# Layer norm of the feed-forward samples by products with a constant tile in place of transposes and batch-norm statistics

## The chip, the cores and the metric

The kernel runs on one core of one Trainium2 chip. The metric is device time in microseconds for one execution. A profile of one execution shows how long each engine worked and what it waited for: TensorE (PE; PEld is its weight load), VectorE (DVE), ScalarE (ACT), GpSimd (POOL) and SyncE (SP), which issues the transfers.

## The reference

A stack of four layers works on x of shape (8, 512, 512): a rotation of columns, a conditioned two-matrix block, a low-rank addition, and a transformer layer. The change lies in the second layer norm of the transformer layer, ahead of its feed-forward part:

```python
def layernorm(x, gamma, beta):
    mu = jnp.mean(x, axis=-1, keepdims=True)
    var = jnp.var(x, axis=-1, keepdims=True)
    return (x - mu) * jax.lax.rsqrt(var + EPS) * gamma + beta
...
x1 = x + attn_out
h2 = layernorm(x1, gamma2, beta2)
ff = jax.nn.gelu(h2 @ W1 + b1, approximate=False) @ W2 + b2
x2 = x1 + ff
g = gate_score[:, None, None]
return x + g * (x2 - x)
```

For each sample there are 512 tokens of 512 features, and the feed-forward part has 2048 hidden features.

## The kernel before

A sample lies in SBUF by features: 128 partitions, J = 4 tiles of 512 tokens, so that feature sums run over the partitions and the tiles. The first third of the run is the conditioned block, the middle is attention of all eight samples, and from about 925 us on only the feed-forward part of the samples is left. The code numbers samples from 0. Sample 0 uses a plain first product, the others (1 to 7) seven block products in place of eight (`product`, `PRODUCTS`), each of two times three passes in 128x256 pieces. The norms that the change touches are those of samples b = 2 to 7, the third to the eighth.

The work of one sample is cut into eight **periods**, p = 0 to 7. In one period TensorE issues, in this order: products 1 and 6 of the next pair of hidden tiles, `second_product` of the first hidden tile on output tiles 0 and 1, product 7, the same `second_product` on tiles 2 and 3, products 4 and 5, `second_product` of the other hidden tile on 0 and 1, products 2 and 3, and `second_product` on 2 and 3. Each half of a `second_product` is six 128x512 matmuls (L83 to L85, the helper `three_pass`). Each engine has its queue in program order, and semaphores tie them. Up to sample 2's statistics and norm the order is written out by hand, one call per line, for each engine; from then on it is the functions `period` in a loop over b = 2 to 7, which prepare sample b + 1 inside sample b.

Between the products of a pair and its `second_product` lies a chain over two engines. DVE adds the products (`partial_of`, L2237). ScalarE applies Gelu (`pair_high`, L2398) and rounds a copy to the matmul's type (L2401). DVE subtracts to get the low part (`pair_low`, L2216). `second_product` waits for that subtraction. `pair_high(n + 1, True)` waits for the fourth partial, `partial_of(n + 1, 3)`; a `product(·, 7)` waits for all five partials of the pair before, and a `product(·, 4)` for the first of its own pair.

The norm of sample b + 1 goes like this. In p = 1 DVE starts the result (`start_result`, L2156) and GpSimd adds a bias to it (L2097). In p = 2 DVE adds the attention result to x (`add_attention`, L2144). At the end of p = 2 and in the middle of p = 3 TensorE transposes x in sixteen 128x128 pieces (`tokens`, L2451) into the two PSUM banks `turn(0)` and `turn(1)`, DVE takes `bn_stats` and `bn_aggr` of each of four token tiles (`statistics`, L2164 and L2166), and GpSimd makes the reciprocal root of four columns by a power of minus a half (L2100, L2102). In p = 4 TensorE spreads mean and reciprocal root over the partitions by eight transposes (`spread`, L2467 and L2471), and DVE subtracts the mean (`centre`, L2177). In p = 5 DVE multiplies by the reciprocal root (`normalise`, L2183), ScalarE scales (`scale`, L2354), and both split the blocks for the products.

For b = 2 the same steps stand in the hand-written queues. ScalarE's is, around the change:

```python
ff.factor_high(6, 0)
ff.pair_high(3, True)
ff.factor_high(6, 1)
...
ff.pair_high(4, False)
ff.factor_high(7, 0)
ff.factor_high(7, 1)
ff.scale(2, 0)
ff.pair_high(5, True)
ff.scale(2, 1)
ff.copy_first(6)
```

`factor_high(6, 0)` and `factor_high(7, 0)` wait for a transfer of weights.

Of the kernel before, what the change touches and what calls it, by code (L numbers as in the profile page):

```python
# [18 lines left out]
P = 128  # L19
# [1906 lines left out]
def feed_forward_engines(nc, ctx, io, keep, psum, attention):  # L1926
# [29 lines left out]
    whole_tile = keep["stack_f"][1][:, 7, :]  # L1956
    partial = rows_of(keep["raw"][:, 2:4, :, :])[:, 6:8, :].rearrange("p n (h s) -> p (n h) s", h=2)
# [16 lines left out]
    added, summed, biased, gated = sem("added"), sem("summed"), sem("biased"), sem("gated")  # L1974
    given_ld, factor_sum, factor_hi, factor_lo = sem("given_ld"), sem("factor_sum"), sem("factor_hi"), sem("factor_lo")
# [30 lines left out]
    made_of = lambda part: given[part[1]][:, :, part[2], :].rearrange("p k a c -> p a k c")  # L2006

# [85 lines left out]
    def gpsimd(pool):  # L2093
        for b in range(B):
# [3 lines left out]
            if b + 1 < B:  # L2098
                pool.wait_ge(mv_set, T * (b + 1))
                pool.tensor_scalar(var[:], mv[:, :, 1], LN_EPS, None, ALU.add).then_inc(var_set, 1)  # L2100
                pool.wait_ge(var_set, b + 1)
                pool.tensor_tensor(rstd[:], var[:], keep["minus_half"][:], ALU.pow).then_inc(rstd_set, 1)  # L2102

    def vector(dve):
# [54 lines left out]
        def statistics(b, t):  # L2159
            if b == 1:  # L2160
                dve.wait_ge(tok_set, t + 1)
            else:
                dve.wait_ge(tin_full, T * (b - 1) + t + 1)
            dve.bn_stats(st[:, t, :], tok[:, t, :] if b == 1 else turn(t)).then_inc(stat_set, 1)  # L2164
            dve.wait_ge(stat_set, T * (b - 1) + t + 1)
            dve.bn_aggr(mv[:, t, :], st[:, t, :]).then_inc(mv_set, 1)  # L2166

# [6 lines left out]
        def centre(b):  # L2174
            dve.wait_ge(tback_full, J + 2 * (b - 2) + 1)
# [71 lines left out]
        def period(b, p):  # L2247
# [7 lines left out]
            if more and p == 3:  # L2255
                statistics(b + 1, 0)
                statistics(b + 1, 1)
# [15 lines left out]
            if more and p == 2:  # L2273
                add_attention(b + 1)
            if more and p == 5:
# [8 lines left out]
            if more and p == 3:  # L2284
                statistics(b + 1, 2)
                statistics(b + 1, 3)
# [21 lines left out]
        return steps(w1_low, w2_low, factor_low, factor_sums, add_attention, start_result, statistics, normalise_first, block_low, block_sums,  # L2308
                     split, finish, pair_low, partial_of, centre, normalise, samples)

    def scalar(act):
# [29 lines left out]
        def tokens(t):  # L2341
# [3 lines left out]
            act.activation(tok[:, t, :], turn(t), ACT.Copy).then_inc(tok_set, 1)  # L2345

# [56 lines left out]
        def period(b, p):  # L2403
# [29 lines left out]
        return steps(w1_high, w2_high, factor_high, tokens, scale, block_high, gelu, copy_first, pair_high, samples)  # L2433

    def tensor(pe):
        def tokens(b, t):
            if t == 0:
                pe.wait_ge(mid_set, J * b)
                if b == 1:
                    attention["results_taken"](pe)  # L2440
                elif b == 2:
                    pe.wait_ge(h_set, J)
                else:
                    pe.wait_ge(normed, T + 2 * J * (b - 2))
# [2119 lines left out]
```

## Time and profile before

| | us |
|---|---|
| median of three runs | 1609.24 |
| the three runs | 1609.21, 1609.24, 1613.74 |
| span of the profiled execution | 1610.9 |
| TensorE busy in it | 1585.8 (98%) |
| VectorE, ScalarE, GpSimd busy in it | 1166.6, 982.8, 410.9 |
| one steady sample (1213.0 to 1299.6) | 86.6 |

The profile gives the span from the first to the last instruction, 1610.9 us, and no separate time for what lies around it. It is 1.7 us above the median and between the runs shown. In a row of the timeline the first number is the start in us, the second the duration; x4 is four instructions shown as one row. Matmuls overlap in the records, so their pace is read from start to start.

### The profile page before, as it was taken

Reading aid. Unit: us, or ns where it says so; the run is one execution under the profiler, and the core shown is the slowest. Engines: PE = TensorE matmul, PEld = TensorE weight load, DVE = VectorE, ACT = ScalarE, POOL = GpSimd, SP = SyncE. Lnnn points to the kernel's source line nnn. Section 1 sums busy time; section 2 is a strip of 40 time slices with the busy share of each in tenths; the row PEclk is TensorE's granted clock in tenths of the full one; section 3 lists DMA queues with packets and bytes.
Section 4 is the critical chain, followed back from the end, with each engine's and each line's share of the span. In section 5 each row is a group of like instructions: output and inputs, shape, how many; then the busy total and the mean of one; then the engine's idle time right before and its main releaser. Section 6 shows DMA issues by size and latency. Waiting matters only on the chain.

```text
span 1610.9 us, 27177 instructions
## 1 busy us (share of the span) xinstructions
PE 1585.8 (98%) x9296; PEld 1299.5 (81%) x9298; DVE 1166.6 (72%) x2767; ACT 982.8 (61%) x2331; POOL 410.9 (26%) x605
## 2 busy tenths in 40 slices
PE   7999999999999999999999999999999999999999
PEld 4688786777777777777777688898999999999998
DVE  7999888786969686868778576785655656565643
ACT  6888766887878787878778755352433324242422
POOL 8998810313222313131312110201010110202010
PEclk8999999999999999999999999999999999999999
DMA  7042135543545444444337435866464555556361
GB/s 308 0 183 97 66 126 126 149 130 92 138 95 139 100 115 122 111 116 115 88 90 214 167 152 207 303 262 232 178 234 170 213 225 188 212 178 265 142 211 68
DMA packets 62257, 254.79 MB, mean 158 GB/s; under 512 B 10628, under 2 KB 16004, under 8 KB 46760
## 3 DMA queue, kind: packets, MB, share of 16 engines
q1 hardware_dynamic: 62120, 253.06, 48.2%
q8 instruction: 74, 1.21, 0.3%
q14 instruction: 63, 0.52, 0.1%
HBM read 153.93 MB, written 48.23 MB: 125 GB/s over the span
## 4 chain that ended last, share of the span: by engine, by line
PE 90%; POOL 3%; DMA 2%; DVE 2%; ACT 1%; issue 1%; SPq 1%; POOLq 0%; DVEq 0%; ACTq 0%
PE psum L83 24%; PE psum L84 23%; PE psum L85 23%; PE psum L1529 5%; PE psum L1549 5%; PE psum L1579 4%; PE psum L1470 1%; DMA k_weights<-w_factors 1%; PE psum L1478 1%; PE psum L2451 1%; DMA k_raw<-in_t_w 1%; POOL k_gs_square L252 1%; POOL k_gs_root L247 1%; ACT psum L1229 1%; POOL k_gs_scaled L256 1%
## 5 line engine op out<-in xcount | busy, mean ns | idle before, releaser
L1229 ACT ACTIVATE psum<-psum,b_mx 128x512 f32<-128x512 f32 (+3 forms) x512 | 258.9, 509 | 63.2 <-DVE b_mx L990 62.0
L990 DVE CUSTOM_DVE_ANT_0 psum<-psum,b_mask 128x512 f32<-128x512 f32 (+3 forms) x512 | 244.7, 506 | 53.0 <-PE psum L1529 48.1
L2398 ACT ACTIVATE k_act<-k_stack_f,k_smalls 128x512 f32<-128x512 f32 x112 | 80.9, 722 | 303.6 <-DVE k_stack_f L2237 297.1
L1241 ACT ACTIVATE k_exps<-psum 128x512 f32<-128x512 f32 (+1 forms) x384 | 194.6, 532 | 59.4 <-PE psum L1549 58.1
L864 POOL TENSOR_SCALAR_AFFINE_SELECT k_exps<-k_exps 128x256 f32<-128x256 f32 x256 | 96.4, 413 | 381.0 <-ACT k_exps L1241 379.1
L2097 POOL TENSOR_SCALAR k_result<-k_result,k_pb 128x512 f32<-128x512 f32 x32 | 59.2, 1866 | 434.9 <-DVE k_result L2156 434.9
L2216 DVE TENSOR_TENSOR k_act_lo<-k_act,k_act_hi 128x512 fp32r<-128x512 f32 x112 | 77.2, 690 | 120.6 <-ACT k_act_hi L2401 120.6
L83 PE MATMUL psum<-k_act_hi,k_w_hi 128*128 128x512 f32 x384 | 150.8, 393 | 0.0
L84 PE MATMUL psum<-k_act_lo,k_w_hi 128*128 128x512 f32 x384 | 150.5, 392 | 0.0
L85 PE MATMUL psum<-k_act_hi,k_w_lo 128*128 128x512 f32 x384 | 150.2, 391 | 0.0
L2237 DVE TENSOR_TENSOR k_raw<-psum,k_raw 128x256 f32<-128x256 f32 x168 | 70.5, 421 | 106.0 <-PE psum L85 95.4
L1529 PE MATMUL psum<-k_stack 96*128 96x512 f32 (+3 forms) x512 | 142.6, 330 | 3.1 <-DMA k_stack<-k_samples 2.0
L85 PE MATMUL psum<-k_normed,k_weights 128*128 128x512 f32 (+1 forms) x384 | 144.3, 376 | 0.0
L1549 PE MATMUL psum<-k_stack 98*128 98x512 f32 (+3 forms) x512 | 134.8, 332 | 0.6 <-ACT k_exps L1241 0.3
L83 PE MATMUL psum<-k_normed,k_weights 128*128 128x512 f32 (+1 forms) x320 | 126.0, 394 | 0.0
L84 PE MATMUL psum<-k_normed,k_weights 128*128 128x512 f32 (+1 forms) x320 | 120.0, 375 | 0.0
L1529 PEld LDWEIGHTS psum<-k_stack 96*128 96x128 f32 x512 | 93.6, 190 | 29.9 <-issue 8.8
L1549 PEld LDWEIGHTS psum<-k_stack 98*128 98x128 f32 x512 | 91.0, 189 | 27.7 <-issue 9.6
L1229 ACT ACTIVATION_READ_ACCUMULATOR psum<-psum,b_mx 128x1 f32 x512 | 108.6, 212 | 0.0
L85 PEld LDWEIGHTS psum<-k_act_hi,k_w_lo 128*128 128x128 f32 x384 | 72.1, 188 | 16.2
L85 PEld LDWEIGHTS psum<-k_normed,k_weights 128*128 128x128 f32 x384 | 73.0, 190 | 14.1
L83 PE MATMUL psum<-k_h,k_stack 128*128 128x256 f32 x294 | 82.6, 281 | 0.0
(372 smaller groups left out, 4418.2 us busy)
## 6 DMA issues: line engine op xcount, KB each, us to landing
k_stack<-w_factors SPq DMA_DIRECT2D x35, 1792.0 KB, 7.7
k_stack<-k_samples SPq DMA_DIRECT2D x384, 128.0 KB, 2.4
k_weights<-w_factors SPq DMA_DIRECT2D x17, 1792.0 KB, 7.5
x<-k_tokens SPq DMA_DIRECT2D x10, 1024.0 KB, 4.3
k_tokens<-x SPq DMA_DIRECT2D x8, 1024.0 KB, 5.1
d<-k_result SPq DMA_DIRECT2D x32, 256.0 KB, 2.9
k_raw<-x SPq DMA_DIRECT2D x8, 1024.0 KB, 4.8
k_raw<-d SPq DMA_DIRECT2D x8, 1024.0 KB, 7.1
```

Source lines behind the costliest of these rows:

```text
L83: pe.matmul(out, w_hi, x_hi, start=start and k == 0, stop=False)
L84: pe.matmul(out, w_hi, x_lo, start=False, stop=False)
L85: last = pe.matmul(out, w_lo, x_hi, start=False, stop=stop and k == n - 1)
L864: pool.affine_select(out=own, in_=own, compare_op=ALU.is_ge, fill=0.0, base=0, pattern=[[0, 2], [1, P]], channel_multiplier=-1).then_inc(c ...
L990: last = dve.tensor_tensor_reduce(got, got, mask[:, S - width:S], -INV_SQRT_DH, -2.0 * MASKED, ALU.add, ALU.min, mx[n % 2][:, h, t:t + 1])
L1229: act.activation(sc(n, u)[:, at:at + width], sc(n, u)[:, at:at + width], ACT.Exp, bias=mx[n % 2][:, h, t:t + 1], scale=-1.0, accum_out=sum ...
L1241: act.activation(exps[n % 2][:, h, at:at + width], by_key(n, u)[:, 0:width], ACT.Exp, scale=INV_SQRT_DH).then_inc(k_act, 1)
L1529: last = pe.matmul(sc(n, u)[:, at:at + width], stack[n % 2][0:3 * DH, 2 * h, t * P:(t + 1) * P], stack[n % 2][0:3 * DH, 2 * h + 1, 0:width ...
L1549: last = pe.matmul(by_key(n, u)[:, at:at + width], stack[n % 2][0:3 * DH + 2, 2 * h + 1, j * P:(j + 1) * P], stack[n % 2][0:3 * DH + 2, 2 ...
L2216: dve.tensor_tensor(act_lo[n % 2], act_f[:], act_hi[n % 2].bitcast(F32), ALU.subtract).then_inc(act_lo_set, 1)
L2237: dve.tensor_tensor(out, got, other, ALU.add).then_inc(partial_set, 1)
L2398: act.activation(act_f[:], whole_tile, ACT.Gelu, bias=small(smalls, "b1", 2 * pair % M + second)).then_inc(pair_gelu, 1)
```

## The change

For samples b = 2 to 7 the transposes and the batch-norm statistics go. GpSimd adds the four tiles of x, splits the sum into a high and a low part (`token_sum`), and TensorE multiplies both with a constant tile of 1/512, which gives the mean, already on all partitions, in `turn(0)` (`mean_product`). ScalarE squares the four tiles of x (`squares`), GpSimd adds the squares and splits the sum (`square_sum`), TensorE multiplies again (`square_product`, `turn(1)`). ScalarE squares the mean, DVE makes the variance, ScalarE takes Ln and Exp of it for a rough reciprocal root, and DVE refines that in three instructions. All of this works on 128x512 elements where the statistics before had a column for each token tile.

```diff
 def gpsimd(pool):
+        def token_sum(b):
+            pool.wait_ge(mid_set, J * (b - 1) + 2)
+            pool.tensor_tensor(sum_f, x[:, 0, :], x[:, 1, :], ALU.add).then_inc(sums_set, 1)
+            for j in (2, 3):
+                pool.wait_ge(mid_set, J * (b - 1) + j + 1)
+                wait_sums(pool, b, j - 1)
+                pool.tensor_tensor(sum_f, sum_f, x[:, j, :], ALU.add).then_inc(sums_set, 1)
+            wait_sums(pool, b, 3)
+            pool.tensor_copy(sum_hi, sum_f).then_inc(sums_set, 1)
+            wait_sums(pool, b, 4)
+            pool.tensor_tensor(sum_lo, sum_f, sum_hi.bitcast(F32), ALU.subtract).then_inc(sums_set, 1)
+
+        def square_sum(b):
+            wait_squares(pool, b, 1)
+            pool.tensor_tensor(tok[:, 0, :], tok[:, 0, :], tok[:, 1, :], ALU.add).then_inc(sums_set, 1)
+            for j in (2, 3):
...
+                pool.tensor_tensor(tok[:, 0, :], tok[:, 0, :], tok[:, j, :], ALU.add).then_inc(sums_set, 1)
+            wait_sums(pool, b, 8)
+            pool.tensor_copy(squares_r[:, 1, :], tok[:, 0, :]).then_inc(sums_set, 1)
+            wait_sums(pool, b, 9)
+            pool.tensor_tensor(squares_r[:, 2, :], tok[:, 0, :], squares_r[:, 1, :].bitcast(F32), ALU.subtract).then_inc(sums_set, 1)
...
+            elif b + 1 < B:
+                token_sum(b + 1)
+                square_sum(b + 1)
 def vector(dve):
+        def variance(b):
+            dve.wait_ge(tback_full, J + 2 * (b - 2) + 2)
+            wait_squares(dve, b, J)
+            dve.tensor_tensor(var_f, turn(1), sum_f, ALU.subtract).then_inc(stat_set, 1)
+            wait_statistics(dve, b, 1)
+            dve.tensor_scalar(var_f, var_f, 0.0, LN_EPS, ALU.max, ALU.add).then_inc(stat_set, 1)
+
+        def refine(b):
+            wait_rough(dve, b, 2)
+            dve.tensor_tensor(var_f, var_f, sum_f, ALU.mult).then_inc(stat_set, 1)
+            wait_statistics(dve, b, 3)
+            dve.scalar_tensor_tensor(var_f, var_f, -0.5, sum_f, ALU.mult, ALU.mult).then_inc(stat_set, 1)
+            wait_statistics(dve, b, 4)
+            dve.scalar_tensor_tensor(sum_f, var_f, 1.5, sum_f, ALU.add, ALU.mult).then_inc(stat_set, 1)
...
-            if more and p == 3:
-                statistics(b + 1, 0)
-                statistics(b + 1, 1)
...
+                if more and p == 4:
+                    variance(b + 1)
                 partial_of(n + 1, 1)
...
+            if more and p == 4:
+                refine(b + 1)
...
             if n + 1 < HALF * (B - 1):
                 partial_of(n + 1, 2)
                 partial_of(n + 1, 3)
-            if more and p == 3:
-                statistics(b + 1, 2)
-                statistics(b + 1, 3)
             if more and p == 4:
                 centre(b + 1)
 def scalar(act):
+        def squares(b):
+            for j in range(J):
+                act.wait_ge(mid_set, J * (b - 1) + j + 1)
+                act.activation(tok[:, j, :], x[:, j, :], ACT.Square).then_inc(tok_set, 1)
+        def mean_square(b):
+            act.wait_ge(tback_full, J + 2 * (b - 2) + 1)
+            act.activation(sum_f, turn(0), ACT.Square).then_inc(tok_set, 1)
+        def rough_rstd(b):
+            wait_statistics(act, b, 2)
+            act.activation(sum_f, var_f, ACT.Ln).then_inc(rstd_set, 1)
+            wait_rough(act, b, 1)
+            act.activation(sum_f, sum_f, ACT.Exp, scale=-0.5).then_inc(rstd_set, 1)
...
+            if more and p == 2:
+                squares(b + 1)
+            if more and p == 3:
+                mean_square(b + 1)
+            if more and p == 4:
+                rough_rstd(b + 1)
 def tensor(pe):
+        def mean_product(b):
...
+            wait_sums(pe, b, 5)
+            pe.matmul(turn(0), mean_of[:], sum_hi, start=True, stop=False)
+            pe.matmul(turn(0), mean_of[:], sum_lo, start=False, stop=True).then_inc(tback_full, 1)
+
+        def square_product(b):
+            wait_sums(pe, b, 10)
+            pe.matmul(turn(1), mean_of[:], squares_r[:, 1, :], start=True, stop=False)
+            pe.matmul(turn(1), mean_of[:], squares_r[:, 2, :], start=False, stop=True).then_inc(tback_full, 1)
...
             second_product(at, m[0], 0, 1)
+            if more and p == 4:
+                square_product(b + 1)
             if first:
                 product(n, 7)
             second_product(at, m[0], 2, 3)
             if more and p == 3:
-                tokens(b + 1, 2)
-                tokens(b + 1, 3)
-            if more and p == 4:
-                spread(b + 1)
+                mean_product(b + 1)
...
-            if more and p == 2:
-                tokens(b + 1, 0)
-                tokens(b + 1, 1)
```

In the hand-written queues for b = 2, ScalarE gets `squares(2)` between `factor_high(6, 0)` and `pair_high(3, True)`, and `mean_square(2)` and `rough_rstd(2)` ahead of `factor_high(7, 0)`. DVE's queue becomes:

```diff
     ff.factor_low(6, 3)
+    ff.pair_low(4, False)
+    ff.variance(2)
+    ff.partial_of(5, 1)
     ff.centre(2)
-    ff.pair_low(4, False)
-    for k in range(1, 4):
+    for k in range(2, 4):
         ff.partial_of(5, k)
     ff.factor_low(7, 0)
+    ff.refine(2)
     ff.normalise(2)
     ff.partial_of(5, 4)
     ff.factor_low(7, 1)
     ff.partial_of(6, 0)
     ff.pair_low(5, True)
```

`start_result`, `add_attention`, `centre`, `normalise` and `scale` stay as they are; `normalise` reads its factor from SBUF (`sum_f`) and not from PSUM.

## Rows read from the trace of the kernel before

**Rows 1.** Windows: busy time and count of PE, PEld, DVE, ACT, POOL, granted clock, DMA.

```profile
1213.00:1299.60 86.60, 86.60 (x554) 78.35 (x553) 52.06 (x95) 31.30 (x51) 8.90 (x6) 1.00 0.56 207
```

**Rows 2.** Chain of waits, in order of time: start, length, engine, line, count.

```profile
1213.78 0.87 PE psum L2451 x8
```

**Rows 3.** Timeline of TensorE, sample 5: period 4, first group of period 5.

```profile
1225.79 0.28 PE L83 MATMUL psum<-k_h,k_stack 128*128 128x256 f32 x1
...
1227.20 0.40 PE L83 MATMUL psum<-k_act_hi,k_w_hi 128*128 128x512 f32 x1
...
1228.57 0.28 PE L83 MATMUL psum<-k_h,k_stack 128*128 128x256 f32 x1
...
1238.49 0.40 PE L83 MATMUL psum<-k_act_hi,k_w_hi 128*128 128x512 f32 x1
```

**Rows 4.** Timeline of DVE in the same sample: `start_result`, `pair_low`, `centre`, `pair_low`.

```profile
1196.85 3.08 DVE L2156 SCALAR_TENSOR_TENSOR k_result<-k_raw,k_pb 128x512 f32<-128x512 f32 x4
...
1212.29 0.69 DVE L2216 TENSOR_TENSOR k_act_lo<-k_act,k_act_hi 128x512 fp32r<-128x512 f32 x1 [1.58 <-ACT k_act_hi L2401]
...
1234.07 2.47 DVE L2177 TENSOR_TENSOR k_tokens<-k_raw,psum 128x512 f32<-128x512 f32 x4
...
1236.46 0.68 DVE L2216 TENSOR_TENSOR k_act_lo<-k_act,k_act_hi 128x512 fp32r<-128x512 f32 x1
```

**Rows 5.** Timeline of ACT in period 4: Gelu and its rounded copy.

```profile
1234.25 0.72 ACT L2398 ACTIVATE k_act<-k_stack_f,k_smalls 128x512 f32<-128x512 f32 x1 [6.41 <-DVE k_stack_f L2237]
1235.00 0.64 ACT L2401 ACTIVATE k_act_hi<-k_act 128x512 fp32r<-128x512 f32 x1
```

**Rows 6.** One line's instructions (L458, Sine with one wait): ns min/median/max, first start.

```profile
L458 ACT ACT_TABLE_LOAD  x1: 1283/1283/1283, 0.8 to 0.8; - x1
L458 ACT ACTIVATE k_sines<-k_angle x1: 236/236/236, 7.7 to 7.7; 128x40 f32<-128x40 f32 x1
```

**Rows 7.** One line's instructions (L2397, second wait ahead of Gelu).

```profile
L2397 ACTq EVENT_SEMAPHORE  x112: 17/17/17, 1004.4 to 1601.6; - x112
```

**Rows 8.** Timeline of ACT at the first Gelu: table load and what follows.

```profile
905.77 1.28 ACT L2380 ACT_TABLE_LOAD   x1
907.06 0.69 ACT L2380 ACTIVATE k_act<-psum,k_smalls 128x512 f32<-128x512 f32 x1
```

**Rows 9.** Groups of DVE by shape: a tensor_scalar from SBUF to SBUF.

```profile
L1059 DVE TENSOR_SCALAR k_samples<-k_samples,b_mv,b_rstd 128x512 f32<-128x512 f32 x32 | 16.1, 541 | 0.2
```

**Rows 10.** Groups of POOL by shape: busy us, mean ns, idle before.

```profile
L851 POOL TENSOR_TENSOR k_normed<-k_samples,k_normed 128x512 fp32r<-128x512 f32 x28 | 36.1, 1289 | 2.3
...
L875 POOL TENSOR_TENSOR k_weights<-k_raw,k_weights 128x512 fp32r<-128x512 f32 x4 | 7.9, 2014 | 0.0
```

**Rows 11.** Timeline of TensorE while sample b = 2 is prepared.

```profile
1037.64 0.39 PE L83 MATMUL psum<-k_h,k_weights 128*128 128x256 f32 x1 [0.50 <-DMA k_weights<-w_factors]
...
1042.28 0.48 PE L83 MATMUL psum<-k_act_hi,k_w_hi 128*128 128x512 f32 x1
...
1054.81 0.36 PE L83 MATMUL psum<-k_h,k_stack 128*128 128x256 f32 x1
...
1063.99 0.28 PE L83 MATMUL psum<-k_h,k_stack 128*128 128x256 f32 x1
...
1067.47 0.40 PE L83 MATMUL psum<-k_act_hi,k_w_hi 128*128 128x512 f32 x1
```

**Rows 12.** Timeline of ACT there: Gelu of `pair_high(3, True)`.

```profile
1039.79 0.71 ACT L2398 ACTIVATE k_act<-k_stack_f,k_smalls 128x512 f32<-128x512 f32 x1
```

**Rows 13.** Timeline of DVE there: `pair_low(3, True)`, then after `normalise(2)` the fifth partial.

```profile
1041.26 0.69 DVE L2216 TENSOR_TENSOR k_act_lo<-k_act,k_act_hi 128x512 fp32r<-128x512 f32 x1 [0.92 <-ACT k_act_hi L2401]
...
1061.64 0.68 DVE L2237 TENSOR_TENSOR k_stack_f<-psum,k_raw 128x512 f32<-128x512 f32 x1
```

**Rows 14.** Windows around a pause of TensorE, columns as in rows 1.

```profile
256.00:259.00 3.00, 1.47 (x7) 0.70 (x5) 2.88 (x5) 0.83 (x4) 0.00 (x0) 1.00 0.09 19
259.00:262.60 3.60, 3.58 (x10) 2.94 (x11) 3.54 (x12) 1.86 (x6) 0.00 (x0) 0.53 0.86 187
```

More of the change, by code:

```diff
@@ L2174, in centre @@
         def centre(b):
[L2175 removed]
+            dve.wait_ge(tback_full, J + 2 * (b - 2) + 2)
             for j in range(J):
@@ L2306, in samples @@
                 finish(B - 1, j)
-        return steps(w1_low, w2_low, factor_low, factor_sums, add_attention, start_result, statistics, normalise_first, block_low, block_sums,
+        return steps(w1_low, w2_low, factor_low, factor_sums, add_attention, start_result, statistics, variance, refine, normalise_first, block_low, block_sums,
                      split, finish, pair_low, partial_of, centre, normalise, samples)
@@ L2431, in samples, with tokens @@
                     period(b, p)
-        return steps(w1_high, w2_high, factor_high, tokens, scale, block_high, gelu, copy_first, pair_high, samples)
+        return steps(w1_high, w2_high, factor_high, tokens, squares, mean_square, rough_rstd, scale, block_high, gelu, copy_first, pair_high, samples)
     def tensor(pe):
-        def tokens(b, t):
+        def tokens(t):
             if t == 0:
[L2438 to L2444, printed above, removed]
+                pe.wait_ge(mid_set, J)
+                attention["results_taken"](pe)
             if t >= 2:
-                if b == 1:
-                    pe.wait_ge(tok_set, t - 1)
-                else:
-                    pe.wait_ge(stat_set, T * (b - 1) + t - 1)
+                pe.wait_ge(tok_set, t - 1)
             for j in range(J):
@@ L2563, in samples @@
                     period(b, p)
-        return steps(tokens, back, spread, first_product, second_product, product, samples)
+        return steps(tokens, back, mean_product, square_product, first_product, second_product, product, samples)
     return {"sync": sync, "gpsimd": gpsimd, "vector": vector, "scalar": scalar, "tensor": tensor}
@@ L3219, in vector_tail @@
     ff.w1_low(4)
-    ff.statistics(1, 0)
+    ff.statistics(0)
     ff.split(4)
@@ L3228, in vector_tail @@
     for k in range(1, 4):
-        ff.statistics(1, k)
+        ff.statistics(k)
     ff.split(6)
@@ L3313, in vector_tail @@
     ff.partial_of(3, 4)
-    ff.statistics(2, 0)
-    ff.statistics(2, 1)
     ff.partial_of(4, 0)
@@ L3319, in vector_tail @@
     ff.partial_of(4, 1)
-    ff.statistics(2, 2)
     ff.pair_low(3, False)
@@ L3323, in vector_tail @@
         ff.partial_of(4, k)
-    ff.statistics(2, 3)
     ff.pair_low(4, True)
@@ L3781, in scalar_tail @@
     ff.factor_high(6, 0)
+    ff.squares(2)
     ff.pair_high(3, True)
@@ L3790, in scalar_tail @@
     ff.pair_high(4, False)
+    ff.mean_square(2)
+    ff.rough_rstd(2)
     ff.factor_high(7, 0)
@@ L4388, in tensor_tail @@
     ff.second_product(23, 6, 0, 1)
-    ff.tokens(2, 3)
+    ff.mean_product(2)
     ff.product(5, 1)
@@ L4392, in tensor_tail @@
     ff.second_product(23, 6, 2, 3)
-    ff.spread(2)
+    ff.square_product(2)
     ff.product(5, 7)
```

65 lines of the change are left out of this document (36 added, 29 removed).

## The prediction

> **What bounds the kernel now.** I read the windows first. In the steady samples TensorE is busy for all of the 86.60 us of a sample at granted clock 1.00 [rows 1], while DVE works 60% of it, ScalarE 36% and GpSimd 10%. The chain of waits says the same: through the transposes it stays on TensorE [rows 2]. So the time of the feed-forward part is TensorE's queue plus every pause put into it. The other engines count only through what TensorE waits for, and I read the timelines for how early each of those things is ready.
>
> TensorE's pace, start to start: twelve 128x256 pieces take 1227.20 - 1225.79 = 1.41 us, six 128x512 take 1228.57 - 1227.20 = 1.37, so 0.228 each [rows 3].
>
> **TensorE's own work.** Removed: 24 transposes for each of six samples. Eight take 0.87 [rows 2], so 24 take 2.61. Added: four 128x512 matmuls at 0.228, 0.91. Gain: 1.70 a sample. For the five samples prepared in the loop that is 8.5 us. Sample b = 2 I count by itself below.
>
> **The mean and the sums (p = 2 and 3).** GpSimd gets ten full-tile operations. None like them is in this stage; the nearest is a 128x512 tensor_tensor at 1.29, or 2.01 in the mean where it met DVE work with two SBUF operands [rows 10]. Token sums: 5 x 1.29 to 5 x 2.01 = 6.5 to 10.1. A period is 10.4 (42 pieces at 0.1175, 24 at 0.228). DVE's adds come behind product 7 of p = 2, and `mean_product` stands a period and six 128x512 later, less what DVE takes to begin: 11.2. The sums start when two adds are done, 1.3 on, so they have 9.9: they fit at 1.29 each and are 0.2 late at 2.01. To `square_product` there are 8.8 more: fitting again, or at 2.01 late by 1.5 in all. I take 1.29, the price of operations most like them, and no wait. What is not free: GpSimd's operations may hold up DVE's attention adds and `pair_low` in p = 2, by up to 1.29 each. `pair_low` was over at 1212.98 [rows 4] and wanted one period and eight transposes ahead of 1227.20 [rows 3], at 1215.9; 2.0 are left without the transposes at the end of p = 2, so I put 0.05 a sample on it. The eight DVE statistics that go were off the path. The Trainium skill (SBUF — State Buffer, "Who interferes with whom") says that a DVE instruction with two SBUF inputs contends with a GpSimd instruction that reads SBUF; the mean of 2.01 against 1.29 agrees.
>
> **The variance in p = 4, step by step.** Zero is the start of the period on TensorE, 1225.79.
> - `square_product` starts at 1.41 + 1.37 = 2.78; its second matmul starts at 3.01 and ends about 3.40; with 0.10 from engine to engine DVE starts at 3.50. This wait sits on DVE ahead of `partial_of(n+1, 1)`, which TensorE wants only at 8.1.
> - DVE: subtraction 0.68 [rows 4], chained step 0.04, tensor_scalar 0.54 [rows 9]: 4.76.
> - ScalarE: handoff 0.10, Ln and Exp at 0.63 each (the copy, [rows 5]), chained: 6.16. The Ln needs another table; the load is 1.28 [rows 6, 8]. In the row of the Sine [rows 6] the load ran at 0.8 and the Sine only at 7.7: with one wait, the load goes ahead of the wait. Ln has one wait and ScalarE is idle before it, so this load is hidden. Were it not, add 1.28.
> - DVE `refine`: handoff 0.10, then 0.71 + 0.79 + 0.68, the last two priced by scalar_tensor_tensor (3.08 / 4 = 0.77) [rows 4]: 8.5. Behind it wait `partial_of(n+1, 2)` and `(n+1, 3)`, 0.35 and 0.68 (estimates from the 0.68 of a full tile [rows 13]): the sums for Gelu are ready at 9.5. Before, Gelu started at 1234.25 - 1225.79 = 8.46 with 0.88 of transposes ahead, so this chain is late by about 1.5 against TensorE.
> - Gelu needs its own table again. It has two waits, and the second is an instruction of its own, one for each of the 112 [rows 7]. A load placed right before the Gelu then stands behind that wait. I take it as exposed, 1.28: Gelu from 10.8, copy from 11.6 (0.75 later [rows 5]) to 12.2, `pair_low` 12.3 to 13.0, at TensorE 13.1. `centre` (2.47 for four [rows 4]) ends at 11.9 and is not last.
> - TensorE wants it at 1238.49 - 1225.79 = 12.70 [rows 3], less 0.88 of transposes, plus 0.46: 12.28.
>
> Wait: 0.8 us a sample, against a `pair_low` that was over before (1236.46 + 0.68 = 1237.14, 1.35 early). Five samples: 4.0. With the load hidden `centre` is last and the wait is 0.3; with both loads exposed it is 2.1. Nothing later in p = 5 is late again: the fifth partial is ready at about 13.7, wanted at 14.5.
>
> **Sample b = 2, the hand-written queues.** Here the engines are fuller, for they also split weights.
> - ScalarE runs `squares(2)` ahead of `pair_high(3, True)`, whose Gelu started at 1039.79 [rows 12] after a transfer. Four squares at 0.52 push it to 1041.9. `pair_low` followed at 1041.26 [rows 13], 1.47 after; now 1043.4, ending 1044.05. GpSimd's sums run then (0.35 more by my guess), so 1044.5 at TensorE. It was wanted at 1042.28 [rows 11]; without the transposes TensorE is there at 1041.8, since `product(4, 1)` still waits for its transfer until 1037.64 [rows 11]. Pause 2.7, net +2.2 against before.
> - From there to the next landmark, `product(5, 7)`, TensorE took 1054.81 - 1042.28 = 12.53 and now 11.32 (the same 10.4 for 42 and 24 pieces, plus 0.91 for the four new ones). Net +1.0 at R, the new time of that product.
> - DVE from R on: `pair_low(4, False)` can't start before R + 0.5; then to `partial_of(5, 4)` it does pair_low 0.6, variance 1.25, a partial 0.35, centre 2.42, two partials 0.95, `factor_low` 0.35, refine 2.2, normalise 2.42: R + 11.0, done and seen at 11.7. It was at R + 6.83 before [rows 13]. `product(6, 7)` wants it at R + 9.0 (1063.99 - 1054.81 = 9.18 before [rows 11]). Pause 2.7.
> - ScalarE then has scale(2, 0) from R + 9.2, the table load, Gelu, its copy, scale(2, 1) and `copy_first(6)`, 0.8 + 1.28 + 0.75 + 0.55 + 0.7 + 0.4 by the prices of [rows 5, 8], to R + 13.7; DVE's `partial_of(6, 0)` behind it is seen at R + 14.2, and `product(6, 4)` waits for that 1.8 more. The next landmark, 1067.47 or R + 12.66, comes at R + 17.0: +4.3.
> - So sample b = 2 costs 1.0 + 4.3 = 5.3 us.
> - Pauses this long also cost clock. After TensorE was busy for 1.47 of 3.00 us, the granted clock was 0.53 in the next 3.6 us, half speed for nearly all of it [rows 14]. A fall of about 3.4 us at the half level (1.2 of 2.4 GHz) costs 1.7. I count one for each of the two pauses, the second overlapping the last wait: 2.9.
>
> **Sum.** -8.5 + 4.0 + 0.25 + 5.3 + 2.9 = **+4.0 us** on the 1610.9 of the profiled span. The span stands 1.7 above the median, and I carry the difference over: 1609.24 + 4.0 = about **1613 us**. A measurement of this kernel tells about 0.3%, 4.8 us, from no change; the forecast lies just inside.
>
> **The rivals.**
> 1. *The clock falls in every steady sample.* If a pause of 0.8 is enough, 1.7 x 5 = 8.5 more: 1621.7, slower. For it: [rows 14]. Against it: pauses of 0.5 as before `product(4, 1)` [rows 11] had none. It decides as soon as three of five fall. Chance 0.13.
> 2. *The switch costs more than its load.* If ScalarE also had to drain around a load, for as long as the load again (1.28 [rows 8]), that would stay hidden at Ln and delay each Gelu behind a switch: 6 x 1.28 = 7.7, 1620.8. In the row of the switch [rows 8] the next instruction starts 1.29 after the load's start, so I give it a chance of 0.04. The Trainium skill (ScalarE: Activation LUTs, "What ACT_TABLE_LOAD costs") gives about 2.66 us for every switch, load and drain; this trace shows 1.29.
> 3. *GpSimd is late.* At 2.01 an operation the squares' sums are 1.5 late a sample, and contention delays `pair_low` besides: 1 to 2 us a sample, 1618 to 1623. For it: the dearer of [rows 10], and that every operation here reads two SBUF operands. Against it: only `pair_low` and the adds have two SBUF operands. Chance 0.13.
> 4. *The load ahead of Gelu is hidden too.* Wait 0.3 in place of 0.8, no clock fall but one: 1609 to 1610, no change to be measured. Chance 0.14.
> 5. *The waits are covered.* The steady pause is nil and the sample b = 2 costs under 3: the 8.5 shows, 1600 to 1604, faster. It needs Ln, Exp and refine 1 us shorter than priced, and ScalarE's squares ahead of its transfer. Chance 0.12.
> 6. The forecast, 1609.5 to 1617, 0.44; a third of it beyond +4.8.
>
> Slower by over 0.3%: 0.13 + 0.04 + 0.13 + 0.14 = 0.44. Within: 0.30 + 0.14 = 0.44. Faster 0.12. The range leaves out the best part of rival 5 and the worst of 1 to 3: 1604 to 1622. The likeliest case by itself reaches from 1609.5 to 1617.
>
> **What the profile after would show.** No L2451 in samples 3 to 8 and four 128x512 products each; TensorE pausing about 0.8 a sample, once, at the first 128x512 group of p = 5, released by `pair_low`; twelve more table loads, six of them straight behind the wait of a Gelu; GpSimd's full-tile operations at 1.3 with a few over 2; no pause at `mean_product` or `square_product`; pauses of about 2.7, 2.7 and 1.8 between 1041 and 1071, and two stretches at half clock there. The prediction is wrong if the pauses at p = 5 are nil or over 2 us, or if the hand-written part costs under 3.

## The result: slower by half a per cent

| | us |
|---|---|
| before, median of five runs | 1609.21 (1608.47 to 1613.74) |
| after, median of five runs | 1619.00 (1617.22 to 1623.48) |
| ratio, with its 95% interval | 1.0054 (1.0034 to 1.0075) |
| span of the profiled execution, before and after | 1610.9 and 1621.7 |

The forecast was 1613.0 in a range of 1604 to 1622, with "slower" and "no change to be measured" at 0.44 each. The time is inside the range and on the slower side, but above the forecast's likeliest case (1609.5 to 1617).

The head of the page of the kernel after:

```profile
span 1621.7 us, 27058 instructions
PE 1582.3 (98%) x9176; PEld 1291.2 (80%) x9178; DVE 1179.9 (73%) x2749; ACT 1030.5 (64%) x2391; POOL 477.8 (29%) x654
```

TensorE is busy for 3.5 us less than before and the span is 10.8 us longer: what was gained in work was lost in pauses. The chain of waits over the feed-forward part (925 us on) names them. Columns: what waited and for whom, then us in total, number of waits, the longest.

```profile
PE psum L83 <- DVE k_act_lo L2279: 9.5, 6, 2.5
PE psum L83 <- DVE k_stack_f L2300: 4.2, 2, 3.5
PE psum L83 <- DVE k_raw L2300: 0.3, 1, 0.3
```

Before, the same stretch had one wait, of 0.5 us for a transfer. Now `pair_low` (`k_act_lo`) makes TensorE wait once in each of six samples, and in the hand-written part three partials come late as well (0.70, 3.52 and 0.34 us), the first of them at `product(4, 1)`, where the kernel before waits 0.50 for its transfer. In the windows of two steady samples, the answer to [rows 1], the columns are the stretch and its length, busy time of PE, PEld, DVE, ACT and POOL, the granted clock, the DMA share and GB/s:

```profile
1162.46:1248.80 86.34, 84.88 (x532) 76.37 (x532) 54.23 (x93) 39.25 (x61) 20.07 (x14) 1.00 0.56 208
1248.80:1335.66 86.86, 85.52 (x532) 76.92 (x532) 54.37 (x93) 39.25 (x61) 20.09 (x14) 1.00 0.56 206
```

A sample took 86.60 before and takes 86.60 in the mean of these two. PE is no longer busy for all of it, and the clock is 1.00 in both. GpSimd works 20 us, and nothing waits for it.

**Where the pause of a steady sample comes from.** Three timelines of the kernel after show p = 4, whose first product starts at 1234.91. TensorE, answering [rows 3]:

```profile
1234.91 0.28 PE L83 MATMUL psum<-k_h,k_stack 128*128 128x256 f32 x1
...
1245.78 0.28 PE L83 MATMUL psum<-k_h,k_weights 128*128 128x256 f32 x1
...
1247.07 0.28 PE L85 MATMUL psum<-k_h,k_weights 128*128 128x256 f32 x1
1248.80 0.50 PE L83 MATMUL psum<-k_act_hi,k_w_hi 128*128 128x512 f32 x1 [1.45 <-DVE k_act_lo L2279]
```

DVE, answering [rows 4]:

```profile
1238.32 0.69 DVE L2218 TENSOR_TENSOR k_raw<-psum,k_stack_f 128x512 f32<-128x512 f32 x1 [0.90 <-PE psum L2549]
1239.05 0.43 DVE L2220 TENSOR_SCALAR k_raw<-k_raw 128x512 f32<-128x512 f32 x1
1242.12 0.69 DVE L2225 TENSOR_TENSOR k_raw<-k_raw,k_stack_f 128x512 f32<-128x512 f32 x1 [2.31 <-ACT k_stack_f L2421]
...
1248.06 0.69 DVE L2279 TENSOR_TENSOR k_act_lo<-k_act,k_act_hi 128x512 fp32r<-128x512 f32 x1 [0.47 <-ACT k_act_hi L2477]
```

ScalarE, answering [rows 5]:

```profile
1236.93 1.28 ACT L2419 ACT_TABLE_LOAD   x1
1239.51 0.63 ACT L2419 ACTIVATE k_stack_f<-k_raw 128x512 f32<-128x512 f32 x1 [1.29 <-DVE k_raw L2220]
1240.16 1.28 ACT L2421 ACT_TABLE_LOAD   x1
1241.45 0.63 ACT L2421 ACTIVATE k_stack_f<-k_stack_f 128x512 f32<-128x512 f32 x1
1245.27 1.28 ACT L2474 ACT_TABLE_LOAD   x1 [3.19 <-DVE k_stack_f L2300]
1246.57 0.72 ACT L2474 ACTIVATE k_act<-k_stack_f,k_smalls 128x512 f32<-128x512 f32 x1
```

Read the ScalarE rows for the loads. The first runs at 1236.93, long before Ln has its data: hidden. The third stands behind the wait of Gelu for the partials: exposed. Both were forecast. The second, at 1240.16 between Ln and Exp, was not. The set that is loaded for Ln is evidently not one that serves for Exp as well, so a sample has three loads, eighteen in six samples, and two of the three lie on the path.

The bracket at 1248.80 says 1.45, but the pause costs more. The last piece of the group ahead started at 1247.07, and these pieces start 0.12 apart, so the next was due at about 1247.20 and started 1.6 later. The idle time is counted from a modelled end.

**Sample b = 2** runs through the hand-written queues. The first long pause has two causes: ScalarE's squares ahead of Gelu, and `pair_low` itself, which took 1.35 in place of 0.69 while GpSimd worked. In the rows below the first is DVE's, the others are TensorE's and answer to [rows 11]:

```profile
1044.90 1.35 DVE L2279 TENSOR_TENSOR k_act_lo<-k_act,k_act_hi 128x512 fp32r<-128x512 f32 x1 [3.00 <-ACT k_act_hi L2477]
...
1046.31 0.79 PE L83 MATMUL psum<-k_act_hi,k_w_hi 128*128 128x512 f32 x1 [2.51 <-DVE k_act_lo L2279]
...
1059.28 0.28 PE L83 MATMUL psum<-k_h,k_stack 128*128 128x256 f32 x1
...
1072.05 0.39 PE L83 MATMUL psum<-k_h,k_stack 128*128 128x256 f32 x1 [3.52 <-DVE k_stack_f L2300]
1073.36 0.48 PE L83 MATMUL psum<-k_h,k_stack 128*128 128x256 f32 x1 [0.34 <-DVE k_raw L2300]
...
1077.82 0.40 PE L83 MATMUL psum<-k_act_hi,k_w_hi 128*128 128x512 f32 x1
```

The windows behind the two long pauses, with the columns as above:

```profile
1046.30:1049.70 3.40, 3.39 (x10) 2.81 (x11) 2.92 (x4) 1.63 (x3) 3.26 (x3) 0.51 0.92 291
...
1073.00:1077.00 4.00, 3.66 (x13) 3.16 (x13) 3.45 (x8) 3.02 (x5) 0.00 (x0) 0.57 0.00 0
```

Each pause is followed by a stretch at half clock (1.2 of 2.4 GHz), 3.4 us long by the granted clock of the record.

**The accounts.** I cut the feed-forward part at three points: the first product after TensorE's wait at `product(4, 1)` (the start; before, it waits there for a transfer), the landmark of the prediction ([rows 11], 1067.47; the matmul with the same number counted from the last one), and the last matmul. The first column of times goes to the end of the span.

| kernel | start to end of span | start to landmark | landmark to last matmul |
|---|---|---|---|
| before | 573.3 | 29.8 | 539.3 |
| after | 582.4 | 38.5 | 539.8 |

So 9.1 us were lost from the start on: 8.6 in sample b = 2, and 0.5 in the five steady samples, which were to gain 8.5 - 4.0 - 0.25. The other 1.7 of the 10.8 us between the spans lie ahead of this part, in attention, where the record of this one execution has a stretch of 6.83 us at half clock in place of one of 3.41 before. The medians differ by 9.8. The profiled execution of the kernel after, at 1623.48, was the longest of its five, with the lowest mean granted clock: 0.992, where the others have 0.993 to 0.995. One stretch of 3.41 us at half clock is 0.001 of that mean, so the others had one to three such stretches fewer. Where they lay is not on record, so the 3.4 us of clock counted below in sample b = 2 hold for the profiled execution.

### The profile page after: what moved, and what is told of

It reads as the page before. It is cut to its first block, busy times and chain, and to the rows that moved or that the text cites. A ratio compares the mean times of both kernels' runs of the same rounds, so it can differ in the third digit from the quotient of the medians.

```text
span 1621.7 us, 27058 instructions
## 1 busy us (share of the span) xinstructions
PE 1582.3 (98%) x9176; PEld 1291.2 (80%) x9178; DVE 1179.9 (73%) x2749; ACT 1030.5 (64%) x2391; POOL 477.8 (29%) x654
## 4 chain that ended last, share of the span: by engine, by line
PE 86%; DVE 4%; POOL 3%; ACT 3%; issue 2%; SPq 2%; DMA 1%; DVEq 0%; POOLq 0%; ACTq 0%
PE psum L83 23%; PE psum L84 22%; PE psum L85 22%; PE psum L1549 5%; PE psum L1529 5%; PE psum L1579 5%; PE psum L1470 1%; PE psum L1478 1%; SPq L779 1%; POOL k_gs_square L252 1%; POOL k_gs_root L247 1%; SPq L787 1%; POOL k_gs_scaled L256 1%; POOL k_gs_norms L249 0%; PE psum L1565 0%
## 5 line engine op out<-in xcount | busy, mean ns | idle before, releaser
L2279 DVE TENSOR_TENSOR k_act_lo<-k_act,k_act_hi 128x512 fp32r<-128x512 f32 x112 | 81.9, 731 | 134.3 <-ACT k_act_hi L2477 134.2
L1549 PEld LDWEIGHTS psum<-k_stack 98*128 98x128 f32 x512 | 91.6, 190 | 28.7 <-issue 10.8
L83 PEld LDWEIGHTS psum<-k_act_hi,k_w_hi 128*128 128x128 f32 x384 | 72.7, 189 | 20.7 <-DVE k_act_lo L2279 10.9
```

The source lines that it names most:

```text
L83: pe.matmul(out, w_hi, x_hi, start=start and k == 0, stop=False)
L1549: last = pe.matmul(by_key(n, u)[:, at:at + width], stack[n % 2][0:3 * DH + 2, 2 * h + 1, j * P:(j + 1) * P], stack[n % 2][0:3 * DH + 2, 2 ...
L2279: dve.tensor_tensor(act_lo[n % 2], act_f[:], act_hi[n % 2].bitcast(F32), ALU.subtract).then_inc(act_lo_set, 1)
```

## The experiments

Each was timed beside the kernel before on the same chip, and each is the changed kernel with the edit shown. The expectations count samples from 1: their "sample 3" is sample b = 2. The times:

| kernel | median, us | runs | ratio to before (95%) | start to end | start to landmark | landmark to last |
|---|---|---|---|---|---|---|
| after | 1619.0 | 5 | 1.0054 (1.0034 to 1.0075) | 582.4 | 38.5 | 539.8 |
| e1, one set for Ln and Exp | 1612.4 | 10 | 1.0013 (1.0003 to 1.0022) | 575.0 | 37.4 | 533.5 |
| e2, Gelu's set early | 1615.5 | 6 | 1.0031 (1.0019 to 1.0043) | 578.2 | 37.0 | 537.1 |
| e3, both | 1607.6 | 10 | 0.9982 (0.9973 to 0.9992) | 569.9 | 34.5 | 531.3 |
| e4, b = 2 by the old norm | 1612.1 | 10 | 1.0016 (1.0006 to 1.0026) | 573.5 | 29.5 | 539.9 |
| g1, squares early | 1617.9 | 5 | 1.0036 (1.0023 to 1.0049) | 580.7 | 36.8 | 539.8 |
| g2, Gelu early | 1613.6 | 10 | 1.0017 (1.0005 to 1.0028) | 577.3 | 31.8 | 541.4 |
| g3, e3 + g1 + g2 | 1605.5 | 5 | 0.9956 (0.9943 to 0.9968) | 567.7 | 30.6 | 533.0 |
| h1, g1 with a late sum | 1616.7 | 5 | 1.0038 (1.0021 to 1.0054) | 579.9 | 35.7 | 540.1 |
| h2, g3 with a late sum | 1604.3 | 5 | 0.9957 (0.9942 to 0.9971) | 566.7 | 29.6 | 533.0 |

Compare kernels by the ratios. The last three columns come from one profiled execution each.

### e1: one table set for Ln and Exp

```diff
 def rough_rstd(b):
+    act.preload_act_table_set("natural_log_exp_and_others")
     wait_statistics(act, b, 2)
     act.activation(sum_f, var_f, ACT.Ln).then_inc(rstd_set, 1)
```

> One line ahead of Ln loads the table set that holds both Ln and Exp, so the load between them (1.28 us) goes; the load ahead of Gelu stays. Theory (the loads sit in the chain that pair_low waits for): the pause of TensorE at the start of period 5, 1.35 to 1.45 us in each of five samples, becomes about 0.1; sample 3 keeps its two long pauses, for there refine waits behind centre on DVE. Median 1619.0 - 6.4 = about 1612.6. Rival (centre and the other work of DVE set the pause, the loads are hidden): the pause stays above 0.8 and the median above 1616.

ScalarE's timeline of a steady sample:

```profile
1229.12 1.28 ACT L2418 ACT_TABLE_LOAD   x1
1231.69 0.63 ACT L2420 ACTIVATE k_stack_f<-k_raw 128x512 f32<-128x512 f32 x1 [1.29 <-DVE k_raw L2220]
1232.36 0.63 ACT L2422 ACTIVATE k_stack_f<-k_stack_f 128x512 f32<-128x512 f32 x1
```

Exp follows Ln after 0.67, where it was 1.94. From the landmark on TensorE's part is 6.3 us shorter than after, 1.26 for each of the five samples, the price of one load on the path (1.28). Three of the five steady pauses are gone and two are 0.17. The ratio to before falls from 1.0054 to 1.0013, which is inside the 0.3% that the prediction took as the limit of what can be told. The load between Ln and Exp is thereby shown to be the term that was missing in the steady samples.

### e2: Gelu's set ahead of its wait

```diff
     act.activation(sum_f, sum_f, ACT.Exp, scale=-0.5).then_inc(rstd_set, 1)
+    act.preload_act_table_set("gelu_and_others")
```

> Gelu's table set is loaded right behind Exp, ahead of the wait of the next Gelu; the load between Ln and Exp stays. Theory: pair_low then waits for centre, which ended at 1247.5 where the subtraction began at 1248.06, so the steady pause falls by 0.56 only, to about 0.85; in sample 3 the Gelu behind scale(2, 0) comes 1.28 earlier and with it the second pause. Median 1619.0 - 2.8 - 1.3 = about 1614.9. Rival (a load placed ahead of a Gelu never waits behind its semaphore): nothing changes, 1619.

```profile
1234.52 1.28 ACT L2422 ACT_TABLE_LOAD   x1
1237.71 0.72 ACT L2475 ACTIVATE k_act<-k_stack_f,k_smalls 128x512 f32<-128x512 f32 x1 [1.91 <-DVE k_stack_f L2300]
...
1237.53 2.47 DVE L2240 TENSOR_TENSOR k_tokens<-k_raw,psum 128x512 f32<-128x512 f32 x4
1239.92 0.69 DVE L2279 TENSOR_TENSOR k_act_lo<-k_act,k_act_hi 128x512 fp32r<-128x512 f32 x1
```

In ScalarE's timeline the load now runs while DVE still refines, and Gelu starts as soon as the partial is there. That is worth 2.7 us from the landmark on, 0.55 a sample, and not 1.28: pauses of 0.78 to 0.89 are left at the same place. The prediction had said so of this load (0.8 with it, 0.3 without, because `centre` is then last on DVE), and the two rows of DVE show it: `pair_low` starts as `centre` (L2240) ends. Both loads together (e3) are worth 8.5, 1.70 a sample, which is nearly the 1.26 and 0.55 of the single ones, and not the 2.57 of two loads.

In sample b = 2 the expectation was missed: the pause of 3.52 fell to 3.08 only, not by 1.28. There the moved load stands ahead of `factor_high(7, 0)` in ScalarE's queue, and DVE waits for that ahead of `refine(2)`:

```profile
1059.51 0.43 DVE L2165 TENSOR_TENSOR k_weights<-b_mask,k_weights 128x256 fp32r<-128x256 f32 x1 [0.72 <-ACT k_weights L2396]
```

### e3: both lines

> Both lines of the two kernels before this one. Theory: subtraction ready 0.4 us before TensorE wants it, steady pause 0, second pause of sample 3 shorter by 1.3: 1619.0 - 7.0 - 1.3 = about 1610.7. If GpSimd's work on shared operands had a part in the steady pause, some 0.3 or more of it stays in each sample and the median is above 1612.

The waits of TensorE from 1000 us on:

```profile
PE psum L83 <- DVE k_stack_f L2300: 3.2, 2, 2.3
PE psum L83 <- DVE k_raw L2300: 1.6, 2, 1.4
PE psum L83 <- DVE k_act_lo L2279: 1.3, 1, 1.3
```

All five lie in sample b = 2, and no steady sample has a pause. Here the gain of the change stands bare: 539.3 - 531.3 = 8.0 us, 1.6 for each of five samples, where 1.70 was worked out. The same five samples in the kernel after are 8.5 longer, so their pauses cost 1.7 each. In sample b = 2 start to landmark falls from 38.5 to 34.5, but not all of that is the loads' work. Theirs are the 1.4 by which the pauses of 3.52 and 0.34 shrink (to 2.27 and 0.18). Another 1.2 is the first pause (1.29 in place of 2.51), ahead of any table load, where `pair_low` took 0.69 and not 1.35. And the record has no fall of the clock there, against two in the kernel after. A new pause of 1.41 takes part of it back. So the median came out 3.1 us below the one expected. Two lines turn a kernel that is slower by 0.54% into one at 0.9982.

### e4: sample b = 2 by the old norm

```diff
 # DVE, in the queue of sample b = 1
+ff.old_statistics(0)
+ff.old_statistics(1)
...
+ff.centre(2)
 ff.pair_low(4, False)
-ff.variance(2)
-ff.partial_of(5, 1)
-ff.centre(2)
-for k in range(2, 4):
+for k in range(1, 4):
     ff.partial_of(5, k)
 ff.factor_low(7, 0)
-ff.refine(2)
```

TensorE's transposes, DVE's statistics, GpSimd's power and the spread come back for b = 2 alone. Samples 3 to 7 stay as changed.

> Sample 3 alone gets its statistics and norm as in the kernel before (transposes, bn_stats, spread), samples 4 to 8 keep the change. Theory: sample 3 accounts for 8.6 us of the loss, with both falls of TensorE's clock; the five steady samples about cancel. Median about 1610.4, no half clock after 1000 us. Rival (the steady samples carry the loss): median above 1615.

```profile
PE psum L83 <- DVE k_act_lo L2293: 7.2, 6, 1.5
PE psum L83 <- DMA k_weights<-w_factors: 1.1, 1, 1.1
```

Start to landmark is 29.5 in place of 38.5: the whole loss of that part goes with the change of one sample. The rest is as after: steady pauses of 1.34 and 1.45, and 539.9 from the landmark on. The kernel is level with before within 0.3%. So in these traces the change splits in two: sample b = 2 lost 8.6 to 9.0, and the other five broke even, as 8.0 gained against 8.5 paid. By the ratios the old norm of sample b = 2 gives back less, 6.1 us (1.0054 to 1.0016), and the median is 1.7 above the one expected; the trace of the kernel after is that of its slowest execution.

### g1: ScalarE's squares ahead of its wait for weights

```diff
-ff.factor_high(6, 0)
 ff.squares(2)
+ff.factor_high(6, 0)
 ff.pair_high(3, True)
```

> The changed kernel with one call moved in ScalarE's hand-written queue for sample 3: squares(2) goes ahead of factor_high(6, 0), into the seven us in which ScalarE waits for a transfer. Theory (the four squares behind that transfer push Gelu and pair_low): the first pause of sample 3, 2.5 us at 1046, falls under 0.4; the second stays near 3.5 with its clock fall. Median 1619.0 - 2.3, and 1.7 less again where the first clock fall doesn't come: 1614.5 to 1617. Rival (the pause comes from GpSimd's work on the shared operands of pair_low): 0.7 or more of it stays, as long as GpSimd still adds squares then.

The pause of 2.51 is gone, but in its place stand two, of 0.49 and 1.43 us, both ahead of the landmark, and start to landmark falls only from 38.5 to 36.8. The median that I expected was missed. What came late is on DVE's timeline:

```profile
1040.15 1.59 DVE L2279 TENSOR_TENSOR k_act_lo<-k_act,k_act_hi 128x512 fp32r<-128x512 f32 x1
...
1043.14 1.74 DVE L2165 TENSOR_TENSOR k_stack<-k_early,k_stack 128x512 fp32r<-128x512 f32 x1
...
1045.66 1.40 DVE L2175 TENSOR_TENSOR b_mask<-b_mask 128x256 f32<-128x256 f32 x1
```

`pair_low` takes 1.59, and the splitting of weights (`factor_low`, L2165; `factor_sums`, L2175) 1.74 and 1.40. GpSimd's `square_sum` now runs in that stretch. h1 tests whether that is why.

### h1: the same, and GpSimd's second sum after DVE's work on the weights

```diff
 def square_sum(b):
+    if b == 2:
+        pool.wait_ge(factor_sum, 4 * (MADE_AT[6] + 1))
```

> The kernel with squares(2) early, and besides GpSimd adds the squares of sample 3 only after DVE's factor_sums(6). Theory (GpSimd's additions slow DVE's subtractions with two SBUF operands: L2165 took 1.74 us in place of 0.68 and L2175 1.40 in place of 0.43, and product(4, 2) waits for the partial behind them): those rows are back at 0.7 and 0.43, the pauses of 0.49 and 1.43 us at 1042 and 1048 are under 0.2 each, and the median is some 1.9 lower, 1616.0. Rival (factor_sums is late for the weights' transfer and ScalarE's queue): the pause of 1.4 stays whatever GpSimd does. GpSimd's work then ends near square_product, where up to 0.5 may be lost again.

```profile
1039.44 0.68 DVE L2167 TENSOR_TENSOR k_stack<-k_early,k_stack 128x512 fp32r<-128x512 f32 x1
...
1040.61 0.42 DVE L2177 TENSOR_TENSOR b_mask<-b_mask 128x256 f32<-128x256 f32 x1
```

The same two operations take 0.68 and 0.42 with GpSimd out of the way, and the pauses of 0.49 and 1.43 are gone, which shows the contention. A wait of 0.56 for a transfer of weights stands there instead, and start to landmark falls by 1.2 more. In the medians that can't be seen: 1.0036 and 1.0038, with intervals that overlap.

### g2: Gelu of pair 5 ahead of the finished norm

```diff
 # ScalarE
-ff.scale(2, 0)
 ff.pair_high(5, True)
-ff.scale(2, 1)
 ff.copy_first(6)
+ff.scale(2, 0)
+ff.scale(2, 1)
 # DVE
 ff.refine(2)
-ff.normalise(2)
 ff.partial_of(5, 4)
-ff.factor_low(7, 1)
 ff.partial_of(6, 0)
+ff.normalise(2)
 ff.pair_low(5, True)
+ff.factor_low(7, 1)
```

> The changed kernel with the calls of sample 3 reordered behind refine(2): ScalarE does pair_high(5, True) and copy_first(6) ahead of scale(2, 0), DVE does partial_of(5, 4) and partial_of(6, 0) ahead of normalise(2). Theory (product(6, 7) and (6, 4) wait for what is queued behind normalise and scale): the pauses of 3.5 and 0.3 near 1072 fall under 0.7 in all, and the clock fall behind them goes; the first pause stays. Median 1619.0 - 3.5 - 1.5 = about 1614. Rival (refine itself ends too late): over 1.5 us stay.

What it undoes is seen in the kernel after. Its ScalarE timeline:

```profile
1068.37 0.81 ACT L2430 ACTIVATE k_tokens<-k_tokens,k_smalls 128x512 f32<-128x512 f32 x1 [3.36 <-DVE k_tokens L2246]
1069.20 1.28 ACT L2474 ACT_TABLE_LOAD   x1
1070.49 0.72 ACT L2474 ACTIVATE k_act<-k_stack_f,k_smalls 128x512 f32<-128x512 f32 x1
```

and its DVE timeline:

```profile
1067.64 2.50 DVE L2246 TENSOR_TENSOR k_tokens<-k_tokens,k_stack_f 128x512 f32<-128x512 f32 x4
1071.30 0.69 DVE L2300 TENSOR_TENSOR k_stack_f<-psum,k_raw 128x512 f32<-128x512 f32 x1 [1.17 <-issue]
```

A row marked x4 covers four operations: the first of DVE's `normalise` lets `scale(2, 0)` start at 1068.37, and behind that stand the load and Gelu. `partial_of(5, 4)` on DVE was free to go at 1070.1 but starts at 1071.30: it writes the tile that Gelu reads, so it waits for Gelu, and TensorE waits 3.52 for it. With Gelu ahead of the scaling, the pauses of 3.52 and 0.34 are gone, start to landmark is 31.8, 6.7 less than after, and the record shows no fall of the clock there. Behind the landmark 1.6 is lost again, of which a pause of 0.62 is the largest part, and the steady pauses stay. So the order of queues is worth 5.1 from start to end, and 3.4 if the first fall of the clock (1.7) is left out: it stayed away although the pause ahead of it (2.43) hardly changed. The ratios say 6.0 (1.0054 to 1.0017). Some four to seven tenths of what sample b = 2 lost was an order of queues.

### g3 and h2: everything together

g3 is the changed kernel with both lines of e3 and the moves of g1 and g2. h2 is g3 with h1's wait.

> Both table lines and both moves together. Theory: no pause over 0.5 us is left in sample 3 or in the steady samples; TensorE's gain of 1.6 us a sample shows in full. From the run with both table lines, 1607.6, sample 3 should give 4.6 + 1.4 = about 6 back: 1601.6, faster than the kernel before by 0.5%. If DVE's queue in sample 3 is simply full, pauses move to later products and the median stays above 1605.

> The kernel with both table lines and both moves, and the same later start of GpSimd's sum of squares in sample 3. Theory: the pause of 0.33 goes; nothing else changes by more than 0.3 us: 1605.2 against the 1605.5 of the run without it, within noise, so a version as good as that one, and faster than the kernel before by 0.4%. If GpSimd ends after the place of square_product, a new pause of 0.5 to 1.0 stands there.

TensorE's waits from 1000 us on, in g3:

```profile
PE psum L83 <- DMA k_weights<-w_factors: 1.9, 1, 1.9
PE psum L83 <- DVE k_raw L2300: 0.9, 2, 0.6
```

and in h2:

```profile
PE psum L83 <- DMA k_weights<-w_factors: 2.3, 1, 2.3
PE psum L83 <- DMA k_stack<-w_factors: 0.9, 1, 0.9
PE psum L83 <- DVE k_raw L2302: 0.6, 1, 0.6
```

Both are faster than before by 0.44%, and they can't be told apart: what h2 saves at DVE (0.33) it waits for a transfer (0.92). From start to landmark h2 is 1.0 shorter all the same, because g3 has a stretch at half clock there, behind its wait of 1.86, in the windows view:

```profile
1035.33:1038.74 3.41, 3.41 (x9) 2.63 (x8) 2.53 (x3) 2.18 (x4) 3.22 (x3) 0.50 0.42 181
```

Ahead of the start both wait longer for their weights (1.9 and 2.3) than the kernel before (0.5); the columns above begin behind that wait. The median of g3 is 3.9 above the one expected, and its ratio (0.9956) is nearly the one expected (0.5% faster): the kernel before, timed beside it, had a median of 1612.36. g3 is the simpler of the two, and none found is faster than they are.

## Why the prediction was right in part, and where it failed

The time was in the range; the sum of +4.0 was 5.1 too low. None of the prediction's signs of being wrong came: the steady pauses are neither nil nor over 2 us, and the hand-written part costs over 3. That the range held is in part its width, for it had room for rivals 1 to 3, and none of these is what happened. Term by term:

| term | forecast | measured, start to end | from |
|---|---|---|---|
| TensorE's work, five samples | -8.5 | -8.0 | before against e3, landmark to last |
| steady pauses, five | +4.0 | +8.5 | after against e3 |
| GpSimd holds up DVE, five | +0.25 | no pause | waits of after and e3 |
| sample b = 2 with clock falls | +8.2 | +8.6 | start to landmark |
| sum | +4.0 | +9.1 | |

**The failed step** is the one in "The variance in p = 4" that took Ln and Exp as chained, "at 0.63 each", with one load ahead of both. Exp had a load of its own, 1.28 on the path: eighteen more loads in the run, where twelve were forecast. By the prediction's zero, the start of p = 4 on TensorE, the steps came out so:

| step | forecast | after |
|---|---|---|
| DVE begins the variance | 3.50 | 3.41 |
| Ln starts | 4.86 | 4.60 |
| refine starts | 6.26 | 7.21 |
| Gelu starts | 10.8 | 11.66 |
| `pair_low` starts | 12.3 | 13.15 |
| at TensorE | 13.1 | 13.89 |
| wanted by TensorE | 12.28 | 12.3 |

Up to Ln the chain was 0.26 early: tensor_scalar took 0.43, not 0.54, DVE began 0.09 sooner, and Ln followed 0.03 and not 0.10 behind it. Then the load adds 1.29 (1240.16 to 1241.45), and the rest carries the difference of 0.8 to 0.95 through. The forecast of what TensorE wants was right to a few hundredths. The wait is so 1.6 start to start in place of 0.8, and by e3 1.7 with what follows. The Trainium skill (ScalarE: Activation LUTs, "Table sets: the hidden batching unit") says that ln then exp need one load, as one set has both. Here they took two until e1 named that set; after e1 they took one.

**Gelu's load (rival 4).** The forecast held: in the five steady samples it runs behind the second wait, in sample b = 2 straight behind `scale(2, 0)`, exposed as well, and e2 and e3 show that it costs, 0.55 a sample with the other load in place and 0.44 more than e1 without it. The prediction's price of 0.5 for it (0.8 against 0.3) was about right.

**Rival 2, a drain around each load,** is out: wherever its data are ready, the instruction behind a load starts 1.29 to 1.30 after the load's start (1240.16 to 1241.45, 1245.27 to 1246.57, 1069.20 to 1070.49). The 2.66 us that the Trainium skill gives for a switch (ScalarE: Activation LUTs, "What ACT_TABLE_LOAD costs") is seen in none of them.

**Rival 1, a fall of the clock in every steady sample,** did not come: the granted clock is 1.00 behind each pause of 1.3 to 1.5, in the kernel after as in e4, g1, g2 and h1, though these pauses were nearly twice what I had priced.

**Rival 3, GpSimd late.** It wasn't late: TensorE has no pause at `mean_product` or `square_product`, and the sums were done 2.5 and 5 us before they were wanted (GpSimd's timeline around 1226 and 1233). Its operations took 0.61 to 1.68, and none took the 2 us that were forecast for a few; two of the ten are casts, which read one operand and not two. Its contention is real, though, and it bit where DVE was full, in sample b = 2, by g1 and h1, and not in the steady samples, where it was priced.

**Sample b = 2.** The sum was right at 8.6 against 8.2, and its parts nearly so. The first landmark came +2.3 later (forecast +2.2). To R (`product(5, 7)`, 1059.28) it took 12.97, against 11.32, as the first clock fall (1.65) lies there. From R to the second landmark it took 18.54, +5.9, where 4.3 and 1.2 of clock were forecast. Its reason was given only in part. I had DVE run `normalise` straight into `partial_of(5, 4)`, but that partial also waits for Gelu of its tile, which stands behind `scale(2, 0)` and a load. The pause was 3.52 in place of 2.7, and the next 0.34 in place of 1.8: together 3.9 for 4.5, and the clock fell at the end of them, so that the products up to the landmark ran at half pace. The close match of the sum is partly luck: the two parts err in opposite directions, and it rests on two falls of the clock in the slowest of five executions.

In the first pause GpSimd's share was larger than my guess (`pair_low` took 0.66 more, not 0.35).

**What stays open.** Why a pause of 2.51 us in the kernel after and one of 1.86 in g3 were followed by half clock, and those of 2.62 in e2, 2.43 in g2, 2.30 in h2, 2.27 in e3 and 2.26 in e1 were not, isn't settled. Five executions of one kernel differ in their mean granted clock, so it need not be the kernel that decides. Behind the same pause of 3.5 the stretch at half clock was 3.4 us long in the kernel after and in e1, and 6.8 in g1 and h1. In g3 the stretch from the landmark on is 1.7 us longer than in e3. All of it is lost in the 12 us behind the landmark: 0.9 at the pause of 0.56, counted from start to start, and the rest in smaller delays of TensorE, which the view of waits doesn't name. What they wait for isn't shown.

## What to carry to other kernels

Two functions of ScalarE in a row are not one table set because one set holds both: look in the trace for a load between them, and name the set, ahead of the wait for the data. A load that follows a wait for a partial result stands in full in its engine's chain, but the time that it costs is no more than the pause of the bottleneck behind it, and ends where another chain comes last: the load of Gelu was 1.28 long and worth 0.55. And where a load is moved ahead, ask what stands behind it in the same queue. In a queue written out by hand, a new operation is paid for by everything behind it: ask for each one who waits for the tile's reader as well as for its writer.

## What was unexpected of the hardware

- A table load was put between Ln and Exp in all six samples, 1.28 each. With the set named there was none.
- The clock did not follow the length of a single pause: 1.86, 2.51 and 3.52 us were followed by 3.4 us at half clock, five others of 2.26 to 2.62 were not, and none of the 25 steady pauses of 1.3 to 1.5 in five kernels was.
- GpSimd's adds of one form, 128x512 from SBUF to SBUF, did not all take the same: 1.29 or 1.30 for most, 1.55 to 1.57 for the second add of each sum in every steady sample, and 1.67 or 1.68 for the first add of x. What sets them apart isn't shown. A row marked x2 also holds the 0.14 between its two adds (1.56, 0.14 and 1.30 here, kernel after):

```profile
1220.83 3.00 POOL L2121 TENSOR_TENSOR k_stack_f<-k_stack_f,k_raw 128x512 f32<-128x512 f32 x2
...
1226.25 1.30 POOL L2129 TENSOR_TENSOR k_tokens<-k_tokens 128x512 f32<-128x512 f32 x1
```

- Beside GpSimd's adds, DVE's work on operands in SBUF took up to 2.6 times its time alone (1.74 against 0.68), and on half a tile 3.3 times (1.40 against 0.42). DVE's tensor_scalar on a full tile took 0.43 alone.
